# Audio tower (state-space layers, attention, experts): the squares among the attention features of q and k move from GpSimd to ScalarE

## The chip, the cores and the metric

The kernel runs on one core of one Trainium2 chip. The metric is the device time of one execution in microseconds, taken as the median of several runs. Everything is float32.

## The reference, cut to what matters

```
h = three state-space layers over x                     # (32, 187, 64)
h = h + attention(layernorm(h))
h = h + experts(layernorm(h))                           # 16 experts, the best two weighted

attention:  q, k, v = split(x @ Wqkv.T + b)             # 8 heads of D = 8
            qn = q / |q| * scale * temperature ; kn = k / |k| * scale
            y  = 0.5 * sum_ij qn_i qn_j (sum_n kn_i kn_j v_n)  + linear term + constant term
            y  = y[1:] / y[0] ; out = y @ Wproj.T + b
```

The quadratic term needs, for each token and each head, the products of all pairs of the 8 components of q (and of k). They are symmetric, so 36 of them are enough: 8 squares, 7 products of neighbours one apart, 6 of neighbours two apart, and so on to 1.

## The kernel before, in words

**State-space layers** come first and take the first 344 us of the span. **Attention** follows, in 8 row blocks r = 0 to 7 (`NQ`), each of 8 units of 94 tokens, so a tile of q and k is 94 partitions by 8 units by 8 heads by 8 components: 512 elements for one of them. **Experts** come last, from about 498 us to the end.

Attention is a software pipeline written out by hand. `attention()` on each engine runs over rounds t = 2 to 11, and in a round each engine works on several row blocks: `ln1` = t (first layer norm), `qkvs` = t - 1 (projection, norms and features), `att` = t - 2 (the attention sums of both halves of a block), `ln2` = t - 3 (output projection, second layer norm), `gate` = t - 4 (choice of experts) and `last` = t - 5 (dispatch weights). Each engine's instructions stand in one fixed order; semaphores hold them back.

The features of block r are written into `kF[r % 2]` and `qF[r % 2]`, 45 per head: 36 products and then the 8 components and a one. The 36 products are made by `products` (L1943), one TENSOR_TENSOR for each distance k = 0 to 7, on 512, 448, 384, ... 64 elements. GpSimd calls it for k and then for q of each block in its `attention()` (L1910, L1914). For q of block 0 alone (`EARLY`) VectorE calls it, in `q_products` (L1679). The last nine features are copied by ScalarE, in `k_linear` (L1236) and `q_linear` (L1243), 576 elements each.

Who waits for the features: TensorE's `moments` (L798) for k, and `q_features` (L824) for q, both one round later, on the semaphores of the products (`kf_g`, `qf_g`, `qf_v`) and of the copies (`lin_a`).

The order around the two copies on ScalarE, in a round with everything in it (L1280 to L1312): `moments` eviction (L1261), squares for the norms (`qk_squares`, L1228), gate exponentials (L1274), norms (L1232, L1234), `second_squares` (L1216), four evictions of transposed q features (L1254), `moments` (L1261), `second_deviation` (L1221, L1223), `dispatch_transposed` (L1199), **`k_linear` (L1240)**, `reciprocal` (L1268, L1270), **`q_linear` (L1246)**, `first_squares` (L1204), four more evictions (L1254), `first_deviation` (L1209, L1211), `reciprocal` (L1268, L1270).

VectorE in the same round: bias additions (L1656), `residual` (L1698), logits, norm sums, scaling of k (L1676) and q (L1677), then the gating of one block in fourteen small steps of 128 elements (L1611 to L1634), in between `second_normalized` (L1646), `attend` (L1693) and, late in the round, `first_normalized` (L1641), which needs ScalarE's L1211 of the same round. TensorE's next projection (L795) needs L1641. TensorE's own round goes: projection (L795), `moments` (L810), turned moments (L820), output projection (L867), gates (L873), transposes (L844), `attend` (L858), centring (L762), again transposes (L844), first variance (L774), `attend` (L858).

Block 0 is prepared before the rounds begin: its `k_linear` runs at the end of the state-space part and its `q_linear` as the first thing in ScalarE's `attention()`.

Of the kernel before, what the change touches and what calls it, by code (L numbers as in the profile page):

```python
# [6 lines left out]
ACT = mybir.ActivationFunctionType  # L7
# [15 lines left out]
H, D = 8, 8  # L23
# [18 lines left out]
HF = QUAD + D + 1  # L42
# [51 lines left out]
def program(nc, a, out):  # L94
    SCALE = float(D) ** 0.25
    with ExitStack() as ctx:
# [21 lines left out]
        delta, u = (big[:, at:at + 750 * RING] for at in (13500, 18750))  # L118
# [66 lines left out]
        def pick(at, rows, n, count=2):  # L185
            return [big[0:rows, at + n * j:at + n * j + n] for j in range(count)]

        qkv = [t.rearrange("p (u w) -> p u w", w=QKVW) for t in pick(0, TP, QU * QKVW)]
        qF, kF = ([t.rearrange("p (u f) -> p u f", f=FEATS) for t in pick(at, TP, QU * FEATS)] for at in (9216, 3456))
# [185 lines left out]
        def after(eng, sem, value):  # L375
            if value > 0:
                eng.wait_ge(sem, value)
# [628 lines left out]
        def _(act):  # L1006
# [121 lines left out]
            def period(n):  # L1128
# [50 lines left out]
                if n == LAST:  # L1179
                    first_squares(0)  # L1180
                    first_deviation(0)
                elif n == LAST + 1:
                    qk_squares(0)
                    first_squares(1)
                    qk_norms(0)
                    first_deviation(1)
                    k_linear(0)
# [48 lines left out]
            def k_linear(r):  # L1236
                act.wait_ge(nrm_v, r * NRV + 4)
                act.wait_ge(ones_g, 1)
                after(act, kv_p, 2 * (r - 1))
                act.activation(kF[r % 2].rearrange("p u (h f) -> p u h f", f=HF)[:, :, :, QUAD:HF],  # L1240
                               qkv[r % 2][:, :, 72:144].rearrange("p u (h d) -> p u h d", d=D + 1), ACT.Copy).then_inc(lin_a, 1)

            def q_linear(r):  # L1243
                act.wait_ge(nrm_v, r * NRV + 5)
                after(act, qt_p, 2 * FTN * (r - 1))
                act.activation(qF[r % 2].rearrange("p u (h f) -> p u h f", f=HF)[:, :, :, QUAD:HF],  # L1246
                               qkv[r % 2][:, :, 0:72].rearrange("p u (h d) -> p u h d", d=D + 1), ACT.Copy).then_inc(lin_a, 1)

# [27 lines left out]
            def attention():  # L1276
                act.wait_ge(xa_g, UNITS)
                act.wait_ge(more_g, MG[NP])
                q_linear(0)
                for t in range(2, PERIODS):  # L1280
                    ln1, qkvs, att, ln2, gate, last = stages(t)
# [17 lines left out]
                    if qkvs is not None:  # L1299
                        k_linear(qkvs)  # L1300
                    if att is not None:
                        reciprocal(2 * att)
                    if qkvs is not None:
                        q_linear(qkvs)
# [40 lines left out]
        def _(v):  # L1345
# [333 lines left out]
            def q_products(r):  # L1679
                after(v, qt_p, 2 * FTN * (r - 1))  # L1680
                products(v, qF[r % 2], heads(r, 0)).then_inc(qf_v, 1)
# [104 lines left out]
        def _(pool):  # L1786
# [111 lines left out]
            def attention():  # L1898
                pool.wait_ge(xa_g, UNITS)
                pool.wait_ge(more_g, MG[NP])  # L1900
                for t in kvm:
                    ins = pool.memset(t[:, :, :, 1, :], 0.0)
                ins.then_inc(kz_g, 1)
                for r in range(NQ):
                    def heads(at):
                        return of_heads(qkv[r % 2], at, H)

                    pool.wait_ge(nrm_v, r * NRV + 4)
                    after(pool, kv_p, 2 * (r - 1))
                    products(pool, kF[r % 2], heads(72)).then_inc(kf_g, 1)  # L1910
                    if r not in EARLY:
                        pool.wait_ge(nrm_v, r * NRV + 5)
                        after(pool, qt_p, 2 * FTN * (r - 1))
                        products(pool, qF[r % 2], heads(0)).then_inc(qf_g, 1)  # L1914
# [27 lines left out]

def products(eng, dst, t):  # L1943

    at = 0
    for k in range(D):
        m = D - k
        ins = eng.tensor_tensor(dst.rearrange("p u (h f) -> p u h f", f=HF)[:, :, :, at:at + m],  # L1948
                                t[:, :, :, 0:m], t[:, :, :, k:D], ALU.mult)
        at += m  # L1950
    return ins
# [87 lines left out]
```

## Time and profile before

| | |
|---|---|
| median of 3 runs | 777.77 us (773.8 to 778.9) |
| time of the profiled execution | 776.19 us |
| its span | 774.3 us |
| TensorE (matmul) busy | 695.7 us, 90% |
| VectorE busy | 533.5 us, 69% |
| ScalarE busy | 433.4 us, 56% |
| GpSimd busy | 441.6 us, 57% |
| `products` on GpSimd | 120 instructions, 89.0 us |
| `products` on VectorE | 8 instructions |

The span runs from the first to the last instruction; the 1.9 us beside it lie outside. Busy time is summed over the whole span, so the share of an engine says little about a stage of 130 us like attention. PE is TensorE, DVE VectorE, ACT ScalarE, POOL GpSimd. Two instructions that follow each other on an engine may overlap by some 0.1 us, so what an instruction adds to a full engine is the distance from its start to the next one's start, not its duration.

### The profile page before, as it was taken

The page shows a single profiled execution, that of the slowest core. Times are in us where ns is not written, and L with a number is a line of the kernel's source. Part 1 is how long each engine was busy: PE and PEld are TensorE (multiplying, and loading weights), DVE is VectorE, ACT ScalarE, POOL GpSimd, SP SyncE. Part 2 cuts the span into 40 slices and gives each one's busy share as a digit, 9 for nine tenths or more (in the row PEclk, how much of TensorE's full clock was granted, in tenths as well). Part 3 has the DMA queues.
Part 4 walks back from the last instruction along what each step waited for, and adds up shares of the span by engine and source line. Part 5 has one row for each costly group of instructions (what it writes and reads, how often), then busy time and mean ns, then how long its engine had stood idle before and what let it go on. Part 6 is the DMA issues. An engine that isn't in the chain of part 4 may idle for free.

```text
span 774.3 us, 11938 instructions
## 1 busy us (share of the span) xinstructions
PE 695.7 (90%) x3858; PEld 329.0 (42%) x3858; DVE 533.5 (69%) x844; ACT 433.4 (56%) x795; POOL 441.6 (57%) x410
## 2 busy tenths in 40 slices
PE   5689999999999997857988888789999999999997
PEld 2344444544545453425566666423333333333332
DVE  3399899989989899584488886494444445444443
ACT  1688777868687875633655654653333333434342
POOL 1388777878787776854776666334344444444440
PEclk9999999999999999776999997999999999999999
DMA  4366564535545444313000000645944533543300
GB/s 132 123 156 156 130 160 127 124 84 132 123 127 125 120 113 100 75 39 78 2 2 4 4 5 5 139 83 105 186 85 107 107 78 83 107 107 84 82 1 20
DMA packets 30061, 70.06 MB, mean 90 GB/s; under 512 B 4564, under 2 KB 20136, under 8 KB 29608
## 3 DMA queue, kind: packets, MB, share of 16 engines
q1 hardware_dynamic: 29688, 68.58, 37.7%
q8 instruction: 34, 0.56, 0.3%
q10 hardware_dynamic: 304, 0.63, 0.2%
q14 instruction: 35, 0.29, 0.1%
HBM read 66.77 MB, written 2.43 MB: 89 GB/s over the span
## 4 chain that ended last, share of the span: by engine, by line
PE 44%; DVE 6%; ACT 3%; issue 1%; DMA 1%; POOL 0%; SPq 0%; DVEq 0%; POOLq 0%; ACTq 0%
PE pair L881 22%; PE pair L965 11%; PE pair L795 3%; ACT big L1254 2%; PE pair L844 2%; PE pair L810 2%; PE pair L858 1%; DMA big<-dispatched 1%; PE pair L762 1%; PE pair L820 1%; PE pair L867 1%; PE pair L873 1%; DVE big L1615 1%; DVE big L1616 1%; DVE big L1623 0%
## 5 line engine op out<-in xcount | busy, mean ns | idle before, releaser
L1772 DVE TENSOR_TENSOR hidden<-pair,tmp 128x502 f32<-128x502 f32 (+1 forms) x192 | 121.6, 675 | 126.9 <-PE pair L881 101.1
L1922 POOL TENSOR_TENSOR hidden<-xs,big 128x502 f32<-128x502 f32 (+1 forms) x96 | 111.8, 1165 | 165.9 <-PE pair L881 143.9
L1321 ACT ACTIVATE tmp<-pair 128x502 f32<-128x502 f32 (+1 forms) x192 | 102.5, 586 | 155.1 <-PE pair L881 155.1
L1948 POOL TENSOR_TENSOR big<-big 94x512 f32<-94x512 f32 (+3 forms) x120 | 89.0, 776 | 44.7 <-DVE big L1676 44.7
L881 PE MATMUL pair<-xs,w 64*128 64x502 f32 (+1 forms) x384 | 106.5, 631 | 0.0
L881 PE MATMUL pair<-hidden,w 64*128 64x502 f32 (+1 forms) x384 | 97.8, 585 | 5.5 <-DVE hidden L1772 3.3
L1466 DVE TENSOR_TENSOR_SCAN pair<-tmp,pair 128x750 f32<-128x750 f32 (+1 forms) x56 | 95.9, 1712 | 8.5 <-ACT tmp L1055 8.2
L1794 POOL TENSOR_TENSOR big<-big,work 128x750 f32<-128x750 f32 (+1 forms) x28 | 45.7, 1634 | 80.2 <-ACT big L1029 80.2
L965 PE MATMUL pair<-hidden,w 128*64 128x502 f32 (+1 forms) x384 | 91.1, 596 | 0.0
L523 PE MATMUL pair<-big,work 128*128 128x512 f32 x112 | 61.5, 631 | 3.7 <-DVE work L1478 3.6
L881 PEld LDWEIGHTS pair<-hidden,w 64*128 64x128 f32 x384 | 36.6, 187 | 51.9 <-issue 46.1
L881 PEld LDWEIGHTS pair<-xs,w 64*128 64x128 f32 x384 | 29.2, 185 | 65.8 <-issue 36.3
L1459 DVE TENSOR_TENSOR pair<-pair,big 128x750 f32<-128x750 f32 (+1 forms) x56 | 51.9, 927 | 2.0 <-PE pair L524 1.9
L1055 ACT ACTIVATE tmp<-big,picked 128x749 f32<-128x749 f32 (+2 forms) x56 | 49.7, 909 | 2.5 <-issue 2.4
L965 PEld LDWEIGHTS pair<-hidden,w 128*64 128x64 f32 x384 | 23.4, 136 | 61.9 <-DVE hidden L1772 34.8
L1797 POOL TENSOR_TENSOR work<-work 128x750 f32<-128x750 f32 (+1 forms) x28 | 46.2, 1649 | 3.7 <-ACT work L1044 3.7
L1804 POOL TENSOR_TENSOR big<-big 128x750 f32<-128x750 f32 (+1 forms) x28 | 46.7, 1668 | 1.7 <-issue 0.9
L1799 POOL TENSOR_TENSOR big<-big,work 128x750 f32<-128x750 f32 (+1 forms) x28 | 46.1, 1646 | 2.2
L523 PE MATMUL pair<-big,quad 128*128 128x512 f32 x56 | 33.1, 675 | 11.3 <-DVE work L1451 10.8
L598 PE MATMUL pair<-tmp,packed 128*128 128x375 f32 (+1 forms) x96 | 35.7, 493 | 0.0
L598 PE MATMUL pair<-work,packed 128*128 128x375 f32 (+1 forms) x96 | 35.6, 492 | 0.0
L858 PE MATMUL pair<-big 90*32 90x188 f32 x512 | 25.0, 338 | 11.0 <-ACT big L1254 11.0
(199 smaller groups left out, 1221.4 us busy)
## 6 DMA issues: line engine op xcount, KB each, us to landing
big<-dispatched SPq DMA_DIRECT2D x40, 502.0 KB, 6.6
spread<-rowsd SPq DMA_DIRECT2D x48, 375.0 KB, 5.7
spread<-rowsd SPq DMA_DIRECT2D x48, 187.5 KB, 3.4
big<-in_x SPq DMA_DIRECT2D x12, 375.0 KB, 6.3
big<-dispatched SPq DMA_DIRECT2D x8, 498.0 KB, 5.8
spread<-rowsd SPq DMA_DIRECT2D x8, 374.0 KB, 5.4
w<-in_w SPq DMA_DIRECT2D x5, 512.0 KB, 7.1
big<-in_x SPq DMA_DIRECT2D x1, 1500.0 KB, 8.3
```

Source lines behind the costliest of these rows:

```text
L523: pe.matmul(dst[:, 0:512], lhsT, rhs[:, 0:512], start=True, stop=True)
L598: mm = pe.matmul(parts(bank[1], l), ident, t, start=(part == 0 and k == 0), stop=(part == 1 and k == 1))
L881: pe.matmul(dst[:, 0:hi - lo], weights[blk, HID * e:HID * e + HID], x[blk, :], start=True, stop=True)\
L965: mm = pe.matmul(bank[4][64 * b:64 * b + 64, 0:hi - lo], w3[:, e, :], hidT[(2 * expert + b) % 8][:, 0:hi - lo], start=(e == 0), stop=(e == ...
L1055: act.activation(seqs(dA[j], l)[:, :, 1:], seqs(of(delta, n), l)[:, :, 1:], ACT.Exp, scale=picked[p % 2][:, j:j + 1]).then_inc(dk_a, 1)
L1321: act.activation(sT[i % 4][:, 0:w], bank[BANK1[i]][:, 0:w], ACT.Silu).then_inc(silu_a, 1)
L1459: v.tensor_tensor(bu, bu, of(u, n), ALU.mult).then_inc(bu_v, 1)
L1466: v.tensor_tensor_scan(h, dA[j][:, 0:w], h, 0.0, ALU.mult, ALU.add).then_inc(sc_v, 1)
L1772: v.tensor_tensor(hidT[i % 8][:, 0:hi - lo], bank[BANK2[i]][:, 0:hi - lo], sT[i % 4][:, 0:hi - lo], ALU.mult)\
L1804: pool.tensor_tensor(of(u, n), of(delta, n), x, ALU.mult).then_inc(u_g, 1)
L1922: pool.tensor_tensor(xw[e % 4][:, 0:hi - lo], xs[:, lo:hi], wx[:, e, 0:hi - lo], ALU.mult)\
L1948: ins = eng.tensor_tensor(dst.rearrange("p u (h f) -> p u h f", f=HF)[:, :, :, at:at + m], t[:, :, :, 0:m], t[:, :, :, k:D], ALU.mult)
```

## The change

ScalarE makes the squares (distance 0) as an activation of kind Square ahead of the two copies, from the same scaled q and k, into the same places. `products` leaves distance 0 out, on GpSimd and, for q of block 0, on VectorE. The copies' semaphore increments stand behind the squares on the same engine, so the readers' waits are unchanged.

```diff
@@ k_linear(r), ScalarE
                 after(act, kv_p, 2 * (r - 1))
+                act.activation(kF[r % 2].rearrange("p u (h f) -> p u h f", f=HF)[:, :, :, 0:D], of_heads(qkv[r % 2], 72, H),
+                               ACT.Square)
                 act.activation(kF[r % 2].rearrange("p u (h f) -> p u h f", f=HF)[:, :, :, QUAD:HF],
                                qkv[r % 2][:, :, 72:144].rearrange("p u (h d) -> p u h d", d=D + 1), ACT.Copy).then_inc(lin_a, 1)
@@ q_linear(r), ScalarE
                 after(act, qt_p, 2 * FTN * (r - 1))
+                act.activation(qF[r % 2].rearrange("p u (h f) -> p u h f", f=HF)[:, :, :, 0:D], of_heads(qkv[r % 2], 0, H),
+                               ACT.Square)
                 act.activation(qF[r % 2].rearrange("p u (h f) -> p u h f", f=HF)[:, :, :, QUAD:HF],
                                qkv[r % 2][:, :, 0:72].rearrange("p u (h d) -> p u h d", d=D + 1), ACT.Copy).then_inc(lin_a, 1)
@@ products(eng, dst, t)
-    at = 0
-    for k in range(D):
+    at = D
+    for k in range(1, D):
         m = D - k
         ins = eng.tensor_tensor(dst...[:, :, :, at:at + m], t[:, :, :, 0:m], t[:, :, :, k:D], ALU.mult)
```

## Rows read from the trace of the kernel before

**Rows 1.** Chain of waits in order of time, round 7: start us, us, what

```profile
439.25 1.53 PE pair L795 x4
...
446.61 0.98 PE pair L844 x12
...
447.70 0.26 ACT big L1216
...
451.02 0.55 DVE xs L1646
...
456.41 0.56 DVE big L1641
457.01 1.53 PE pair L795 x4
```

**Rows 2.** Timeline, ScalarE, round 6: start us, us, instruction [idle before <-releaser]

```profile
426.01 1.04 ACT L1228 ACTIVATE big<-big 94x1024 f32<-94x1024 f32 x1
...
432.65 0.52 ACT L1223 ACTIVATE xs<-xs 128x376 f32<-128x376 f32 x1
...
433.43 0.70 ACT L1240 ACTIVATE big<-big 94x576 f32<-94x576 f32 x1
434.03 0.29 ACT L1268 ACTIVATE big<-pair 128x188 f32<-128x188 f32 x1
...
434.62 0.72 ACT L1246 ACTIVATE big<-big 94x576 f32<-94x576 f32 x1
435.23 0.46 ACT L1204 ACTIVATE big<-pair 128x376 f32<-128x376 f32 x1
435.59 1.58 ACT L1254 ACTIVATE big<-pair 90x376 f32<-90x376 f32 x4
...
437.66 0.52 ACT L1211 ACTIVATE big<-big 128x376 f32<-128x376 f32 x1
```

**Rows 3.** Timeline, VectorE and TensorE, round 6

```profile
431.83 1.01 DVE L1611 SCALAR_TENSOR_TENSOR big<-big,ridx 94x128 f32<-94x128 f32 x1
...
433.26 0.55 DVE L1646 TENSOR_TENSOR xs<-pair,xs 128x376 f32<-128x376 f32 x1
...
438.65 0.55 DVE L1641 TENSOR_TENSOR big<-pair,big 128x376 f32<-128x376 f32 x1
...
437.42 1.48 PE L858 MATMUL pair<-big 90*32 90x188 f32 x32 [0.63 <-ACT big L1254]
```

**Rows 4.** Timeline, GpSimd, round 6: the first product, then all sixteen

```profile
431.16 1.54 POOL L1948 TENSOR_TENSOR big<-big 94x512 f32<-94x512 f32 x1 [5.76 <-DVE big L1676]
...
431.16 11.98 POOL L1948 TENSOR_TENSOR big<-big 94x512 f32<-94x512 f32 x16 [5.76 <-DVE big L1676]
```

**Rows 5.** Timeline, ScalarE and VectorE, ends of rounds 2, 3 and 4

```profile
364.82 0.33 ACT L1268 ACTIVATE big<-pair 128x188 f32<-128x188 f32 x1 [1.51 <-PE pair L858]
...
369.02 0.55 DVE L1641 TENSOR_TENSOR big<-pair,big 128x376 f32<-128x376 f32 x1 [3.02 <-ACT big L1211]
...
385.38 0.55 DVE L1641 TENSOR_TENSOR big<-pair,big 128x376 f32<-128x376 f32 x1 [3.21 <-ACT big L1211]
...
401.92 0.52 ACT L1211 ACTIVATE big<-big 128x376 f32<-128x376 f32 x1
...
403.14 0.55 DVE L1641 TENSOR_TENSOR big<-pair,big 128x376 f32<-128x376 f32 x1
```

**Rows 6.** Timeline, VectorE, start of round 2: the squares of q of block 0

```profile
352.16 0.68 DVE L1948 TENSOR_TENSOR big<-big 94x512 f32<-94x512 f32 x1
```

**Rows 7.** Timeline, TensorE, ScalarE and VectorE, end of round 8

```profile
472.56 1.76 PE L858 MATMUL pair<-big 90*32 90x188 f32 x32 [2.00 <-ACT big L1254]
...
474.78 0.36 ACT L1270 ACTIVATE big<-big 128x188 f32<-128x188 f32 x1
...
475.86 0.34 DVE L1693 TENSOR_TENSOR big<-pair,big 128x188 f32<-128x188 f32 x1
```

**Rows 8.** Stage table: from:to, us, busy us by engine, granted TensorE clock, DMA

```profile
474.20:484.00 9.80, 8.71 (x92) 6.67 (x84) 4.43 (x13) 1.86 (x5) 4.45 (x7) 0.51 0.01 2
```

## The prediction

> **What bounds the kernel now.** The change touches attention alone, 344 to 498 us of the span, so I read the chain of waits there first, in order of time. It repeats with a period of 17.76 us (L795 to L795) [rows 1]. The reader is to see how the chain is passed on in a round: TensorE without a gap from L795 to the transposes L844; ScalarE from L1216 to L1223; VectorE from L1646 through the gating to L1641; TensorE again. GpSimd is not on it. So the engine that is relieved is not the bound, and the question is how near ScalarE and VectorE run to each other at the end of a round.
>
> The timelines of the engines in round 6 answer that. **GpSimd** makes its sixteen products in 11.98 us, from 431.16 to 443.14 [rows 4]. q's eight come last, and the transposes that read them are still running at 446.61 in the next round (L844, [rows 1]); k's eight come first and are done about halfway. GpSimd has several microseconds to spare, and what it saves is worth nothing by itself. **ScalarE** has no idle time from L1223 to L1211: each row begins where the last one ends, but for the overlap [rows 2]. Both copies lie in that stretch, and so will both squares. L1211 ends at 438.18 (437.66 + 0.52) [rows 2]. **VectorE**'s L1641, which needs it, starts at 438.65 [rows 3]. The hand-over takes 0.09 us: L1223 ends at 433.17 [rows 2], and L1646, which waits for it, starts at 433.26 [rows 3]. So ScalarE has 438.65 - 438.18 - 0.09 = 0.38 us to spare in rounds 5 to 7, which look alike.
>
> In the other rounds it has less, or a little more. In rounds 2 and 3 no block is gated, VectorE waits 3.02 and 3.21 us for L1211 [rows 5], and ScalarE has nothing to spare. In round 4 there is gating but no L1199 yet: L1211 ends at 402.44 and L1641 starts at 403.14 [rows 5], 0.61 us to spare.
>
> **What a square costs on ScalarE.** The trace shows no square of 512 elements with these strides. Nearest are the copy of 576 elements, same tiles and strides, which takes 0.70 us and holds the engine for 434.03 - 433.43 = 0.60 us, the square of 376 elements, which holds it for 435.59 - 435.23 = 0.36 us, and the square of 1,024, 1.04 us long [rows 2]. 512 lies between 376 and 576: not below 0.36, not above 0.60. I take 0.54, near the copy, which has the same source and shape; from 576 to 512 elements the slope between the two squares ((1.04 - 0.46) / 648 = 0.9 ns an element) takes off 0.06. No table load is added: squares of this kind already stand among Ln and Exp with none between. Two squares a round: **1.08 us**, bounds 0.72 and 1.20.
>
> The Trainium skill, page "ScalarE: Activation LUTs", section "What ACT_TABLE_LOAD costs", gives 186 ns + 0.833 ns an element with 93 ns of overlap between neighbours; an estimate from it is 0.52 us for a square, and the sum below would be 0.3 us smaller. Its section "Rules for kernel authors" puts multiplications on VectorE rather than ScalarE, which speaks against this change; no row here tests that choice.
>
> **Part by part, for the end of the kernel.**
> - *Start of round 2.* VectorE's eight products for q of block 0 lie on the chain, since TensorE waits for what VectorE does behind them. The square, 0.68 us long [rows 6], goes; less the overlap that is **-0.60** (bounds -0.68 and 0, if the stage after it takes the gain back). ScalarE was idle when block 0 was prepared, so its two squares there cost nothing; without that cover they would cost 1.08.
> - *Round 2.* The square of k is hidden, since ScalarE waits 1.51 us for TensorE's L858 behind its copy of k [rows 5]. That of q is not: **+0.54**. Bounds 0.36 and 0.60.
> - *Round 3.* Both squares, nothing to spare: **+1.08** (0.72 to 1.20).
> - *Round 4.* 1.08 less 0.61: **+0.47** (0.11 to 0.59).
> - *Rounds 5 to 7.* 1.08 - 0.38 = 0.70 each, **+2.10** (1.02 to 2.46). Behind the squares on ScalarE are the evictions L1254, for which TensorE's L858 waits. In round 6 that is at 437.42, to 438.90 [rows 3]; moved by the full 1.08 it ends at 439.98. The next L795 moves from 439.25 [rows 1] to 439.95 for L1641's sake. TensorE thus becomes free just as L1641 ends, and this second path adds 0.03 at most. The reciprocals at the end of a round move by 1.08 as well, VectorE's L1693 behind them by 0.70; the same pair has some 0.6 to spare in [rows 7], which covers the rest.
> - *Round 8.* No L1641. L858 starts at 472.56 after 2.00 us of waiting for L1254 [rows 7] and moves by 1.08. Its reciprocal ends at 475.14 and VectorE takes it at 475.86 [rows 7], about 0.6 to spare, so 0.5 remains; but L858 would run fully in the stretch of half clock that begins near there [rows 8], up to 0.8 more. I take **+0.90** (0.1 to 1.4).
> - *GpSimd.* Fourteen instructions a round in place of sixteen, the first of which took 1.54 us [rows 4]: 0 on the chain.
>
> Sum: -0.60 + 0.54 + 1.08 + 0.47 + 2.10 + 0.90 = **+4.5 us**, bounds +1.6 and +6.3. Against the profiled execution (776.19 us) that is 780.7; its time is 1.6 below the median of the runs, so against the median it is **782.3**.
>
> **Rival 1, VectorE gains more than ScalarE loses.** VectorE's small steps are stretched while GpSimd works. L1611, on 128 elements, takes 1.01 us, longer than VectorE's 0.68 for 512 [rows 6], and ends at 432.84 [rows 3], just after GpSimd's first product ends at 432.70 [rows 4]. Several of the small steps end some 0.14 us behind a GpSimd product in this way. Two products fewer a round leave less to wait for, and VectorE comes to L1641 earlier. It can gain no more than ScalarE's own time to spare, since then L1641 waits for L1211: 0.61 in round 4 and 0.38 in rounds 5 to 7, 1.75 in all, and only where the squares cost nothing. The rival decides where the two squares together add less than 0.38 us, 0.19 each. At its end it gives -1.75 - 0.60 = -2.35: **775.4** against the median. Against it: 0.19 is below the shortest bound, 0.36. For it: the stretched steps are plain in the rows, and if ScalarE's overlaps swallow more than I think, this is where the time goes.
>
> The Trainium skill, page "SBUF — State Buffer", section "SBUF: two separate sides", says that a VectorE instruction with two SBUF inputs and a GpSimd instruction take a shared port pair as an exclusive lock, for the whole instruction. The trace agrees, with ends 0.14 us apart. By that rule alone the change would be a gain, as in this rival.
>
> **Rival 2, TensorE's clock falls in more rounds.** Place: TensorE waiting for L1254 before L858. In round 8 it stood idle for 2.00 us there [rows 7], and the stage from 474.2 to 484.0 has a granted clock of 0.51, the lower level of 1.2 GHz, with TensorE busy for 8.71 of 9.80 us [rows 8]. The change adds up to 1.08 us of idle time at the same place in rounds 3 to 7, where the clock is full now. At double speed the 8.71 us would take 4.36, so one fall costs at most 4.4 us. It decides from the first extra fall: one gives 782.3 + 4.4 = **786.7**, two 791. Against it: TensorE is still busy before and behind the gap, and its round has only one gap of that kind.
>
> The Trainium skill, page "TensorE: Matmul & The Clock Gate", Part 1, says the clock follows how busy TensorE has been recently; rows here show only that a wait of 2 us stood before a fall.
>
> **Rival 3, nothing moves.** The squares overlap with waits for TensorE that I read as hand-overs (as in round 4), and only rounds 2 and 3 and the start count: about +1, **779**.
>
> **How the numbers follow.** Forecast 0.60, rival 1 0.10, rival 2 0.18, rival 3 0.12. The three runs before span 5 us, so the median itself can shift by some 2 us. Against the median the sum's bounds are 779.4 and 784.1. Toward rival 1's 775.4 below, and past one fall of the clock (786.7) above, that makes 776 to 788; a second fall and the far end of rival 1 are left out. A difference of about 1%, 7.8 us, is what a measurement can tell from none: below 770.0 nothing but a lucky clock leads, 0.02; above 785.5 lead most of rival 2 (0.12) and the dear end of the forecast (0.05), 0.17; within, 0.81.
>
> **What would show it.** In the changed trace: the two new activations on ScalarE at about 0.54 us from start to start; VectorE idle before L1641 with ScalarE's L1211 as releaser in rounds 4 to 7 too; a period of 18.4 to 18.5 us; VectorE's gating over sooner; GpSimd under 10.5 us a round; L858 in rounds 5 to 7 waiting 1 us longer. I am wrong if the squares cost under 0.4, if the period stays at 17.8, or if a round shows a half clock.

## The result and the profile after

The changed kernel takes **784.64 us** (median of 16 runs, 778.57 to 789.28) against 775.12 us for the kernel before (16 runs, 770.64 to 778.99). The ratio is **1.0107, 95% interval 1.0086 to 1.0129**: 8.3 us slower (6.7 to 10.0; the two medians are 9.5 us apart), where I had forecast 4.5 us slower, 782.3 on a median then given as 777.77. The time lies in the range of 776 to 788, and the sign is the forecast one. The size is about double the forecast and beyond the bounds of its sum (+1.6 to +6.3). That the time still comes within 2.3 us of 782.3 is partly luck, since the median that I started from was 2.7 us too high. The experiments divide the loss, to within some 2 us: about 4 us are the squares on ScalarE, as worked out, and about as much is TensorE's clock, which I had as a rival.

The page of the changed kernel, span and busy time of the engines:

```profile
span 782.9 us, 11938 instructions
## 1 busy us (share of the span) xinstructions
PE 702.2 (90%) x3858; PEld 331.7 (42%) x3858; DVE 532.3 (68%) x843; ACT 442.5 (57%) x811; POOL 426.9 (55%) x395
```

ScalarE has 16 instructions and 9.1 us more, GpSimd 15 and 14.7 us less. The span is 8.6 us longer than the 774.3 of the kernel before.

The timeline of ScalarE in round 6 of the changed kernel, which answers to [rows 2] (columns as there; L1240 and L1248 are the new squares, L1242 and L1250 the copies, L1272 is the former L1268 and L1258 the former L1254):

```profile
434.96 0.65 ACT L1240 ACTIVATE big<-big 94x512 f32<-94x512 f32 x1
435.51 0.69 ACT L1242 ACTIVATE big<-big 94x576 f32<-94x576 f32 x1
436.10 0.29 ACT L1272 ACTIVATE big<-pair 128x188 f32<-128x188 f32 x1
...
436.70 0.66 ACT L1248 ACTIVATE big<-big 94x512 f32<-94x512 f32 x1
437.25 0.70 ACT L1250 ACTIVATE big<-big 94x576 f32<-94x576 f32 x1
437.84 0.46 ACT L1204 ACTIVATE big<-pair 128x376 f32<-128x376 f32 x1
438.20 1.58 ACT L1258 ACTIVATE big<-pair 90x376 f32<-90x376 f32 x4
...
440.27 0.52 ACT L1211 ACTIVATE big<-big 128x376 f32<-128x376 f32 x1
```

Each square holds the engine for 0.55 us (434.96 to 435.51, 436.70 to 437.25), and nothing around it has become shorter.

VectorE, TensorE and GpSimd in the same round, which answer to [rows 3] and [rows 4] (L1645 is the former L1641):

```profile
440.89 0.55 DVE L1645 TENSOR_TENSOR big<-pair,big 128x376 f32<-128x376 f32 x1 [1.04 <-ACT big L1211]
```

```profile
438.35 0.90 PE L774 MATMUL pair<-big,averaging 128*128 128x376 f32 x2 [0.69 <-ACT big L1204]
440.04 1.48 PE L858 MATMUL pair<-big 90*32 90x188 f32 x32 [0.79 <-ACT big L1258]
441.50 1.53 PE L795 MATMUL pair<-wqkv,big 128*94 128x384 f32 x4
```

```profile
432.68 9.94 POOL L1953 TENSOR_TENSOR big<-big 94x448 f32<-94x448 f32 x14 [8.54 <-DVE big L1680]
```

VectorE had no wait before this instruction in [rows 3] and now waits 1.04 us for ScalarE's L1211. TensorE waits twice on ScalarE and goes from L858 into L795 without a gap. GpSimd needs 9.94 us in place of 11.98 and waits longer.

Then the clock. The chain of waits of the changed kernel at the end of round 7 and in round 8 (start us, us, what):

```profile
441.51 1.51 PE pair L795 x4
...
456.77 1.49 ACT big L1258 x4
...
458.50 2.63 PE pair L858 x32
461.13 2.81 PE pair L795 x4
463.94 1.36 PE pair L810 x32
```

The same 32 matmuls L858 took 1.48 us a round earlier and take 2.63 here. The stage table of the changed kernel for two stretches (columns as in [rows 8]; the number behind POOL's is the granted clock):

```profile
458.20:465.00 6.80, 6.50 (x68) 3.82 (x68) 3.35 (x9) 1.71 (x5) 2.88 (x5) 0.53 0.02 5
479.60:492.60 13.00, 12.30 (x126) 9.62 (x127) 5.28 (x14) 2.34 (x6) 3.14 (x6) 0.50 0.01 1
```

Before, there was one such stretch in rounds 3 to 9, the 9.8 us of [rows 8]. Now there are two, 19.8 us together, both at the lower level of 1.2 GHz, and the second begins behind this wait, which was 2.00 us in [rows 7]:

```profile
479.75 2.74 PE L858 MATMUL pair<-big 90*32 90x188 f32 x32 [3.08 <-ACT big L1258]
```

**Where the 8.6 us of the two traces lie**, from the starts of L795:

| stretch | before | changed | difference |
|---|---|---|---|
| to the projections of block 1 | 347.00 | 346.09 | -0.9 |
| round 2 with its start | 22.62 | 23.00 | +0.4 |
| round 3 | 16.37 | 17.34 | +1.0 |
| round 4 | 17.76 | 18.13 | +0.4 |
| rounds 5 and 6 | 17.75 each | 18.46 and 18.48 | +1.4 |
| round 7 | 17.76 | 19.56 | +1.8 |
| rounds 8 and 9, to the experts' first matmul | 34.60 | 38.81 | +4.2 |
| the rest | 282.7 | 283.0 | +0.3 |

Rounds 3 to 6 are as forecast to 0.1 us each (1.08, 0.47, 0.70, 0.70). Round 7 has 1.1 too much and rounds 8 and 9 have 3.3 more than the forecast 0.9; both are where the stretches of half clock lie.

### The profile page after: what moved, and what is told of

It reads as the page before. It is cut to its first block, busy times and chain, and to the rows that moved or that the text cites. A ratio compares the mean times of both kernels' runs of the same rounds, so it can differ in the third digit from the quotient of the medians.

```text
span 782.9 us, 11938 instructions
## 1 busy us (share of the span) xinstructions
PE 702.2 (90%) x3858; PEld 331.7 (42%) x3858; DVE 532.3 (68%) x843; ACT 442.5 (57%) x811; POOL 426.9 (55%) x395
## 4 chain that ended last, share of the span: by engine, by line
PE 46%; ACT 5%; DVE 3%; issue 2%; DMA 1%; POOL 0%; SPq 0%; DVEq 0%; POOLq 0%; ACTq 0%
PE pair L881 22%; PE pair L965 11%; PE pair L795 3%; ACT big L1258 3%; PE pair L858 2%; PE pair L844 2%; PE pair L810 2%; PE pair L762 1%; DMA big<-dispatched 1%; PE pair L867 1%; PE pair L873 1%; PE pair L820 1%; ACT big L1250 0%; PE pair L756 0%; DVE hidden L1776 0%
## 5 line engine op out<-in xcount | busy, mean ns | idle before, releaser
L1953 POOL TENSOR_TENSOR big<-big 94x448 f32<-94x448 f32 (+6 forms) x105 | 73.8, 739 | 64.9 <-DVE big L1680 64.9
L858 PE MATMUL pair<-big 90*32 90x188 f32 x512 | 27.4, 360 | 13.5 <-ACT big L1258 13.5
```

## The experiments

Each kernel was run in five rounds beside the kernel before, and the ratios are to that.

**1. No squares at all.** The changed kernel without the two activations; nobody makes the squares.

```diff
-                act.activation(kF...[:, :, :, 0:D], of_heads(qkv[r % 2], 72, H), ACT.Square)
-                act.activation(qF...[:, :, :, 0:D], of_heads(qkv[r % 2], 0, H), ACT.Square)
```

> The squares are made by no engine (this part of the computation is left out); GpSimd makes seven products. Theory A (the squares lengthen ScalarE's full stretch, and everything else follows from it): ScalarE is as before, so the whole loss goes: rounds 5 to 7 last 17.76 us or a little less, the total is 772 to 775 us against 775.1 before. VectorE's steps, less held up by GpSimd, may take the rounds down by no more than ScalarE's 0.38 us to spare. Rival B (the loss comes from the other order on GpSimd and VectorE): the rounds stay at 18.4 and the total near 784.

Measured: 772.50 us, ratio 0.9962 (0.9942 to 0.9982). The loss comes from ScalarE's two instructions and not from the new lists on GpSimd and VectorE, which by themselves are a gain of 2.9 us. TensorE's timeline, one round:

```profile
436.13 1.21 PE L795 MATMUL pair<-wqkv,big 128*94 128x384 f32 x3
...
453.67 0.56 PE L795 MATMUL pair<-wqkv,big 128*94 128x384 f32 x1
```

The round takes 17.54 us, 0.2 less than before. Why not the full 0.38, VectorE's timeline of this kernel shows:

```profile
432.57 0.29 DVE L1620 TENSOR_TENSOR big<-big 94x128 f32<-94x128 f32 x1
...
433.72 0.93 DVE L1623 TENSOR_TENSOR big<-big 94x128 f32<-94x128 f32 x1
434.69 0.35 DVE L1693 TENSOR_TENSOR big<-pair,big 128x188 f32<-128x188 f32 x1
434.96 0.53 DVE L1627 TENSOR_TENSOR big<-big 94x128 f32<-94x128 f32 x1
```

L1623 and L1620 are steps on 128 elements, and one is three times as long. GpSimd's shorter list puts its product of 448 elements of q where k's of 64 used to be. L1623 ends at 434.65, 0.15 us behind that product (434.50); in the kernel before it took 0.49 and ended 0.14 us behind the product of 64. Fewer products give back less than their number.

**2. GpSimd's load put back.** The changed kernel with one more product, into free memory, ahead of each set.

```diff
+                    again(2 * r, heads(72))       # 384 elements, distance 2, into hidden
                     products(pool, kF[r % 2], heads(72)).then_inc(kf_g, 1)
```

> The changed kernel, with one more product of 384 elements ahead of each GpSimd set, written to memory that is free then, so that GpSimd again makes sixteen instructions a round and takes about 12 us. Theory A: same time as the changed kernel, 784 us, rounds of 18.4 to 18.5 us, since VectorE waits for ScalarE's L1211 by about 1 us in any case. Rival V (VectorE's relief hides part of the squares' cost): rounds longer by 0.3 us or more, 786 or above.

Measured: 783.20 us, ratio 1.0101 (1.0067 to 1.0135), the same as the changed kernel's 1.0107. No worth of VectorE's relief can be told while ScalarE bounds the round, as theory A (ScalarE's longer stretch is the cause) says, and rounds 3 to 5 take 17.36, 18.13 and 18.47 us, as in the changed kernel. The trace has one thing that the changed kernel's has not: in rounds 6 and 8 the second half of the projection waits 0.58 us for VectorE's bias additions (L1660), which kernel 8 comes back to. It also has a fall of the clock within the rounds, this time near 441 us, in round 6.

**3. The same squares, later in the round.** Their own semaphore; k's behind `first_deviation`, q's behind the last `reciprocal`.

```diff
                     if ln1 is not None:
                         first_deviation(ln1)
+                    if qkvs is not None:
+                        k_squares(qkvs)
                     if att is not None:
                         reciprocal(2 * att + 1)
+                    if qkvs is not None:
+                        q_squares(qkvs)
```

> The changed kernel with the same two squares on ScalarE, but later in the round: k's behind first_deviation, where ScalarE waited 0.84 us for TensorE's L858, q's behind the last reciprocal, where it waited 3.4 to 3.8 us. Theory A: nothing of the two squares is left on the path, rounds 5 to 7 take 17.4 to 17.8 us, total 772 to 775. Rival B' (ScalarE's squares cost by their number, wherever they stand, or features come too late): still above 779.

Measured: 773.31 us, ratio **0.9967** (0.9942 to 0.9992). The same work on the same engine, moved by 4.6 to 4.8 us within the round, turns a loss of 8.3 us into a gain of 2.6. ScalarE's timeline (L1256 and L1262 are the squares, L1284 the reciprocal's first half):

```profile
438.87 0.66 ACT L1256 ACTIVATE big<-big 94x512 f32<-94x512 f32 x1
439.80 0.33 ACT L1284 ACTIVATE big<-pair 128x188 f32<-128x188 f32 x1 [0.27 <-PE pair L861]
...
440.43 0.65 ACT L1262 ACTIVATE big<-big 94x512 f32<-94x512 f32 x1
```

ScalarE waits 0.27 us for TensorE where it waited 0.84: k's square fills that wait. Rounds 5 to 7 are 17.55 to 17.57 us.

**4. The copy of q goes there too.**

```diff
-                    if qkvs is not None:
-                        q_linear(qkvs)            # behind reciprocal(2 * att)
...
                     if qkvs is not None:
+                        q_linear(qkvs)            # behind reciprocal(2 * att + 1)
                         q_squares(qkvs)
```

> As the third kernel, and q_linear's copy also goes behind the last reciprocal. ScalarE's stretch before L1211 is 0.6 us shorter than in the kernel before. Theory A: rounds 2 and 3, where nothing else bounds, 0.6 us shorter each than in the third kernel, rounds 4 to 7 then bounded by VectorE alone, 17.3 to 17.5 us: total 770 to 773. If VectorE is not relieved by fewer GpSimd products, rounds 4 to 7 stay at 17.7 and the total is about 774.

Measured: 773.79 us, ratio 0.9982 (0.9958 to 1.0005): nothing more. The expectation for rounds 2 and 3 was wrong: ScalarE's next instruction, L1208 (`first_squares`), now waits for TensorE's centring (L763). The timeline of round 3 shows it:

```profile
382.08 0.48 ACT L1208 ACTIVATE big<-pair 128x376 f32<-128x376 f32 x1 [0.47 <-PE pair L763]
```

Of the 0.6 us taken off ScalarE 0.47 become that wait, and round 3 stays at 16.36 us. ScalarE and TensorE are balanced there, so only lengthening ScalarE is felt. Rounds 5 to 7 stay at 17.53 to 17.55 us, as in kernel 3; the expected shortening did not come there either.

**5. The clock kept up in the changed kernel.** Matmuls of 376 columns that nobody reads, into a free bank, where TensorE waits: three in round 2, one before `first_variance` of rounds 3 to 7, one before the second `attend` of rounds 2 to 7 and 9, and four before that of round 8.

```diff
+            def fill(t, count):
+                ...
+                for _ in range(count):
+                    pe.matmul(bank[7][:, 0:QC], averaging[:, :], wqkv[:, 0:QC], start=True, stop=True)
```

> The changed kernel, with matmuls that nobody reads put where TensorE waits: three in round 2 ahead of the turned moments, one before first_variance and one before the second attend of rounds 3 to 7, four before the second attend of round 8. ScalarE's path is unchanged. Theory A+C (the squares cost about 4 us through ScalarE's order, and the rest of the 9.5 us through a granted clock that falls while TensorE waits longer): no stretch of half clock from 352 to 490 us, rounds 5 to 7 still 18.4 to 18.5 us each, total 775 to 779. Rival A alone (the rounds' length is the whole cost, the falls of the clock cost nothing because ScalarE bounds): 783 to 785. If the fillers delay TensorE, rounds get longer than 18.5.

Measured: 776.76 us, ratio **1.0006** (0.9987 to 1.0024), 7.8 us less than the changed kernel. TensorE's timeline (L795 is now the filler and L805 the projection), and its stage table for rounds 7 to 9:

```profile
439.94 0.83 PE L795 MATMUL pair<-wqkv,averaging 128*128 128x376 f32 x2
440.80 0.90 PE L774 MATMUL pair<-big,averaging 128*128 128x376 f32 x2
441.54 0.79 PE L795 MATMUL pair<-wqkv,averaging 128*128 128x376 f32 x2
442.48 1.48 PE L868 MATMUL pair<-big 90*32 90x188 f32 x32
443.94 1.53 PE L805 MATMUL pair<-wqkv,big 128*94 128x384 f32 x4
...
462.41 1.53 PE L805 MATMUL pair<-wqkv,big 128*94 128x384 f32 x4
```

```profile
442.00:462.00 20.00, 18.54 (x232) 12.62 (x234) 15.70 (x35) 13.27 (x32) 11.46 (x17) 1.00 0.02 4
462.00:494.00 32.00, 29.21 (x404) 21.17 (x398) 23.94 (x60) 18.15 (x46) 11.52 (x18) 1.00 0.04 13
```

The rounds are still 18.47 us (443.94 to 462.41), so ScalarE's order is untouched, but the clock is full from 372 to 494 us, and rounds 8 and 9 take 31.32 us in place of 38.81. In round 2 the fillers did not help: a stretch at half clock, from 362 to 369.5 us, is still there. How much of this the kernel before would gain as well, the next ones show.

**6. Fillers in the kernel before, in rounds 2 and 8 only.**

```diff
+                    if t == 2:
+                        fill(t, 3)                # ahead of moments_turned(2 * att)
...
+                        if t == 8:
+                            fill(t, 3)            # ahead of attend(2 * att + 1)
```

> The kernel before, with three such matmuls in round 2 and three in round 8, and none elsewhere. If the two half-clock stretches of 350 to 365 us and 474 to 484 us go, up to 8 us of slower matmuls go, less what other engines bound: 768 to 772. If the clock falls all the same, 775. The difference between the changed kernel with fillers and this one is then the squares' own cost, which theory A puts at 4 to 5 us plus the start's 0.6.

Measured: 776.77 us, ratio 0.9983 (0.9954 to 1.0012). No gain that can be told, and the reason is in TensorE's timeline: the filler closed the wait in round 8, and the clock fell behind the next one, in round 9.

```profile
472.97 1.48 PE L868 MATMUL pair<-big 90*32 90x188 f32 x32
474.24 0.84 PE L820 MATMUL pair<-big 94*32 94x90 f32 x32
477.02 1.13 PE L830 MATMUL pair<-ksel,big 128*90 128x128 f32 x4 [1.94 <-DVE big L1701]
```

L830, 0.60 to 0.64 us at full clock, takes 1.13. I had expected 768 to 772 us if both stretches went. So this was no control for kernel 5.

**7. Squares late, fillers in rounds 2 and 8:** the edits of 3 and 6 together.

> The squares late in the round as in the third kernel, with the fillers of the kernel before (rounds 2 and 8 only). Theory A+C: both gains add, 1 to 2 us below the kernel before with fillers, 766 to 770, and rounds of about 17.6 us. Rival: the start's 0.6 us and VectorE's relief are lost among other waits, and it equals the kernel before with fillers.

Measured: 772.52 us, ratio 0.9953 (0.9938 to 0.9968), above the 766 to 770 that I expected. The granted clock stayed full from 367 to 495 us in its trace, with the same fillers with which it fell in kernel 6: whether it falls behind a wait of 1.9 us differs from case to case. Behind 495 us, at the start of the experts, there is a stretch of half clock instead.

**8. Only k's squares on ScalarE.**

```diff
-                act.activation(qF...[:, :, :, 0:D], of_heads(qkv[r % 2], 0, H), ACT.Square)
...
-                        products(pool, qF[r % 2], heads(0)).then_inc(qf_g, 1)
+                        all_products(pool, qF[r % 2], heads(0)).then_inc(qf_g, 1)   # with distance 0
```

> Only k's squares are made by ScalarE; q's stay with GpSimd (and VectorE for block 0). Theory A, from 0.55 us a square: round 2 nothing, round 3 +0.55, round 4 nothing (0.61 to spare), rounds 5 to 7 +0.17 each, round 8 nothing or little: +1 to +1.5 us, 776 to 777, rounds 5 to 7 at 17.9 us. By a cost in proportion to the number of squares (rival), half of 9.5: about 780. If the clock falls in a further round: 779 or more.

Measured: 779.09 us, ratio 1.0033 (1.0015 to 1.0052), that is +2.6 us (1.2 to 4.0), above my +1 to +1.5. Rounds 3 to 5 are as expected (round 5: 17.92 us), but rounds 6 and 7 take 18.54. VectorE and TensorE in that place:

```profile
440.00 0.80 DVE L1632 TENSOR_TENSOR big<-big 94x128 f32<-94x128 f32 x1
...
441.38 0.75 DVE L1636 TENSOR_TENSOR big<-big 94x128 f32<-94x128 f32 x1
...
442.32 1.00 DVE L1658 TENSOR_TENSOR big<-pair,bqkv 94x384 f32<-94x384 f32 x2
```

```profile
440.13 1.53 PE L795 MATMUL pair<-wqkv,big 128*94 128x384 f32 x4
441.59 0.83 PE L810 MATMUL pair<-big 94*32 94x90 f32 x32
443.01 1.50 PE L795 MATMUL pair<-wqkv,big 128*94 128x384 f32 x4 [0.58 <-DVE big L1658]
```

The last gating steps, on 128 elements, run beside q's eight products and are held up to 0.80 and 0.75 us (0.44 and 0.29 in the kernel before); each ends 0.14 to 0.15 us behind one of them. The bias additions behind them come late, and the second half of the projection waits 0.58 us. Here VectorE's delays by GpSimd reach the path behind L1641, a place that I had not looked at. It needs a product in just the wrong position; kernel 2 has it too, and the changed kernel doesn't. Rounds 8 and 9 take 37.15 us in this trace against 34.60 before: the half clock there lasts from 475.5 to 489.5 us, behind a wait of 2.54 us for L1256. So part of the loss is again the clock.

**9 to 11. The control.** The same fillers in rounds 2, 8 and 9 for the kernel before, for the squares placed late, and for the changed kernel (four in round 8).

```diff
+                    if t in (2, 9):
+                        fill(..., 3)              # ahead of moments_turned(2 * att)
...
+                        if t > 7:
+                            fill(t, 3 if t == 8 else 1)
```

> The kernel before with fillers in rounds 2, 8 and also 9 (three ahead of the turned moments, where TensorE waited 1.94 us in the earlier filler kernel, and one before the last attend). If the fall of the clock near 475 us is due to those waits, it goes, and rounds 8 and 9 take 31.3 us as in the changed kernel with fillers, in place of 34.6: total 772 to 774. If the clock falls all the same: 775 to 777.

> The squares late in the round, with the same fillers. Theory A+C: 1 to 2 us below the kernel before with the same fillers, 770 to 772, rounds 4 to 7 at 17.55 us.

> The changed kernel with the same fillers (four instead of three in round 8), and none in rounds 3 to 7. The difference to the kernel before with the same fillers is the squares' own cost plus any fall in rounds 3 to 7. Theory A+C: 776 to 777, as with the fillers in every round, if falls in rounds 3 to 7 are rare; 779 to 781 if they are common, as the one at 458 us in the changed kernel's trace suggests.

Measured: kernel 9 **771.79 us, ratio 0.9952** (0.9931 to 0.9972); kernel 10 772.73 us, 0.9958 (0.9938 to 0.9979); kernel 11 777.78 us, 1.0022 (1.0000 to 1.0044). Rounds 8 and 9, from the last L795 (here L805) to the experts' first matmul (here L891), in kernel 9:

```profile
454.67 1.53 PE L805 MATMUL pair<-wqkv,big 128*94 128x384 f32 x4 [0.36 <-DVE big L1655]
...
485.86 1.11 PE L891 MATMUL pair<-xs,w 64*128 64x502 f32 x4
```

31.19 us, without squares and without a fall; 31.32 in kernel 5, with squares and without a fall. So the squares cost 0.1 us in these two rounds, and what is above 31.2 goes with the half clock: 3.4 us in the trace of the kernel before (34.60), 7.5 in that of the changed kernel (38.81). Kernel 11 has no fillers in rounds 3 to 7, and there its trace has a fall in round 7, as the changed kernel's. Its time lies between my 776 to 777 us (such falls rare) and 779 to 781 (common).

```profile
458.06 2.51 PE L868 MATMUL pair<-big 90*32 90x188 f32 x32 [0.78 <-ACT big L1272]
```

That one fall takes 2.5 us: round 7 lasts 19.43 us and rounds 8 and 9 last 32.90, against 18.47 and 31.32 in kernel 5.

Kernel 10 against 9 (0.9958 and 0.9952) shows no gain of the late squares beyond the fillers, where I expected 1 to 2 us. Its rounds 4 to 7 are 0.2 to 0.3 us shorter each (17.46 to 17.57 us against 17.76 and 17.77), and the intervals would hide such a gain.

Kernel 9 has one thing that kernel 5 has not, behind the rounds. At the start of the experts its clock falls, and from 494 to 504 us it is at 0.51:

```profile
493.75 2.05 PE L891 MATMUL pair<-hidden,w 64*128 64x502 f32 x4 [2.40 <-POOL hidden L1936]
```

From the experts' first matmul to the end it takes 284.1 us and kernel 5 takes 282.2. Kernels 3, 6, 7, 10 and 11 have a fall there too; the kernel before and the changed kernel have none.

**The division.** With the clock kept up in rounds 3 to 9 on both sides, kernel 5 against kernel 9, the squares cost 1.0006 - 0.9952 = 0.0054, **4.2 us** (2.1 to 6.3, by the two intervals). In the two traces rounds 3 to 9 alone differ by 3.5 us (0.97, 0.34, 0.71, 0.70, 0.70 and 0.13). The whole change costs 8.3. The other **4.1 us** go with half-clock time that the changed kernel has more of. Over the runs the mean granted clock is 0.963 in the changed kernel (16 runs) and 0.965 to 0.967 in the kernel before (three groups of 28 or 29 runs). If the clock is half for one hundredth more of 775 us, the mean falls by 0.005; so 0.002 to 0.004 is 3 to 6 us more of it, worth half at most, 1.6 to 3.1 us. By that measure the clock's share is somewhat less than 4.1. Over its runs kernel 9's mean clock (0.974) is also below kernel 5's (0.978), so kernel 9 still has more half-clock time than kernel 5, and the squares' share may be above 4.2. That both parts are there is shown; their sizes are known to some 2 us.

## Why the prediction came out as it did

- **Who bounds.** Right for the changed kernel: ScalarE's stretch up to L1211 and L1258 is on the path, and GpSimd is not. It can come onto it through VectorE, by 0.58 us a round (kernels 2 and 8), which I had not looked for.
- **Price of a square.** 0.54 forecast, 0.55 measured. The Trainium skill's page "ScalarE: Activation LUTs", section "What ACT_TABLE_LOAD costs", gives 0.52 as an estimate, and the measurement is nearer to the 0.54 taken from the copy's row.
- **Start and round 2.** Forecast -0.06 together, measured +0.4 between the two traces. The stretches of half clock there differ from trace to trace, and round 2 took 20.96 us in kernel 9 and 24.15 in kernel 1, both without squares on ScalarE; so half a microsecond can't be told apart there, and this stays open.
- **Rounds 3 to 7.** Forecast 1.08, 0.47 and three times 0.70; measured 1.0, 0.4, 0.7, 0.7, and 0.7 in round 7 of kernel 5. Right. The second path, L858 straight into L795, is the one that the rows show, and it adds no more than the 0.03 us that I gave it (0.70 to 0.73 in rounds 5 and 6).
- **Round 8.** Mis-sized. I took +0.9 for the squares' delay; it is 0.1 with the clock up (kernels 5 and 9) and 4.2 with the clock as it fell. The delay of L858 is there, 3.08 us of wait for 2.00, but the time to spare behind it was larger than I read. I took 0.6 us from a row in which L858 ran partly at half clock (1.76 us); with the clock up it is 1.0 us in kernel 9 (from the end of L1284, 472.54, to VectorE's L1707), and kernel 5, with the squares, has used it up:

```profile
472.18 0.36 ACT L1284 ACTIVATE big<-big 128x188 f32<-128x188 f32 x1
473.55 0.34 DVE L1707 TENSOR_TENSOR big<-pair,big 128x188 f32<-128x188 f32 x1
...
481.01 0.36 ACT L1289 ACTIVATE big<-big 128x188 f32<-128x188 f32 x1
481.40 0.35 DVE L1712 TENSOR_TENSOR big<-pair,big 128x188 f32<-128x188 f32 x1
```

- **Rival 2, the clock.** This is where the prediction fell short: its sum put a further fall of the clock at nothing, and I gave it a chance of 0.18. It came, in round 7, and the one in round 8 became longer (13.0 us for 9.8). By my own signs, "if a round shows a half clock", the forecast's mechanism was incomplete. The three traces of kernels with both squares in the old place and no fillers in rounds 3 to 7 (changed, 2 and 11) have a fall in round 6 or 7; those of kernels without squares there (before, 1, 3, 4, 6, 7, 9 and 10), the one with k's squares alone (8) and the one with fillers (5) have none. A fall took 2.5 us (kernel 11 against 5; in the changed kernel round 7 has 1.1 too much and the stretch runs on into round 8), less than my bound of 4.4. What happened before it is a pair of waits, 0.70 us before L774 and 0.78 before L858, where there were 0.63 before L858 and 0.35 before L795; so the delay was split, and L858 did not wait 1 us longer, as I had said it would. The same pair stands in rounds 5 and 6 of the changed kernel without a fall, so it doesn't decide by itself; what does stays open. The Trainium skill, page "TensorE: Matmul & The Clock Gate", Part 1, has the clock follow recent activity; kernel 5, with the waits filled, agrees.
- **Rival 1, VectorE's relief.** Real but 0.2 us a round rather than 0.38, and seen only where ScalarE's stretch is as before (kernels 1 and 3). The lock in the Trainium skill, page "SBUF — State Buffer", section "SBUF: two separate sides", agrees again with kernels 1 and 8, where one step among equal ones is 0.4 to 0.6 us longer and ends 0.14 to 0.15 us behind a GpSimd product.
- **Rival 3** is out: the squares were felt in each of rounds 3 to 7.

**A better version.** The squares late in the round (kernel 3, 773.3 us) beat both kernels, the kernel before by 0.0033. The kernel before with fillers (kernel 9, 771.8 us, ratio 0.9952) is the fastest of those run, together with kernels 7 and 10.

## What to carry to other kernels

Before work is moved to an engine that is idle for 44% of the time, look at where in its order it would stand: the same two activations cost about 4 us ahead of a chain of evictions and nothing that could be told behind it, where the engine waits anyway (kernel 3, 0.9967, against 0.9962 without any squares). Measure the time to spare at the wait that ends the round, in hundredths of a microsecond, on each of the engines that meet there. And where the delay falls on TensorE, add to the sum what its clock may do; here that was about as much as the delay itself.

## What the runs showed of the hardware that I had not expected

- A small VectorE step was held until a GpSimd product had ended (0.14 to 0.15 us before the step's own end), so its length depends on which product is running: L1623 took 0.49 us before and 0.93 in kernel 1, L1630 and L1634 0.44 and 0.29 before and 0.80 and 0.75 in kernel 8. Taking products away can make a given step longer.
- Matmuls without use can pay: with one to four of them of 0.7 to 0.8 us at a wait, 3.7 us (kernel 9), and 7.8 us in the changed kernel (kernel 5). With one wait closed, the fall of the clock can come behind the next one (kernel 6, 1.94 us in round 9; kernel 9, 2.40 us in the experts, though kernel 3 has a fall there without fillers).
